# An attention and gated feed-forward layer on eight cores: the up-weight loads go from GpSimd's DMA queue to ScalarE's

## The chip, the cores and the metric

One Trainium2 chip, all eight cores. Each core takes one of the eight sequences (4096 tokens of 1024 features) through the whole layer by itself; the cores exchange nothing. The metric is the device time of the slowest core, in microseconds (us).

## The reference

```python
x = L0_attn_x                                  # (8, 4096, 1024), float32
xn = _layernorm(x, axis=-1)
s = attn(xn, Wq, bq, Wk, bk, Wv, bv, Wo, bo)   # 16 heads of 64, rotary q and k, causal softmax
# feed-forward, 3072 hidden; the weights are integers times 1/127
gate = einsum('bsd,hd->bsh', xn, w_gate / 127)
up   = einsum('bsd,hd->bsh', xn, w_up / 127)
h    = silu(gate) * up
g    = silu(einsum('bsh,dh->bsd', h, w_down / 127))
out  = x + s * g
```

## The kernel before

The kernel is written engine by engine: a small scheduler class (`Sched`) appends each instruction to its engine's list, with the semaphores that it waits for, and every DMA goes through one helper, so that all of them carry line 99 in the profile. An engine works through its list in the order written, and a DMA whose wait is not yet met holds up all that stands behind it in the list of the engine that issues it. SP, ACT and POOL issue DMAs. The helper's first argument names the issuing engine.

There are three parts.

1. Layer norm of x, 32 tiles of 128 tokens, transposed into `xnT`.
2. Attention for eight pairs of heads. In this part POOL also converts the integer feed-forward weights to bf16, in DRAM, into `wsc` (72 DMAs, 24 for each of gate, up and down).
3. The output projection, the feed-forward net and the final product, eight tiles of 512 tokens (`it`). This is the part that the change touches. Its SBUF tiles are carved out of `SCR` and `xnT`, and the profile calls them by these two names. In it the weights come from `wsc` by DMA, again for every token tile, each kind into a pair of slots:
   - gate weights of hidden chunk `hc` (256 KB, `wg_sl`), issued by ACT;
   - up weights (256 KB, `wu_sl`), issued by POOL;
   - the two halves of the down weights (128 KB each, `wdA_sl` and `wdB_sl`), issued by SP, which also loads x and stores the result.

Within one token tile the order is as follows.

- **Loop A**, 24 hidden chunks (lines 839 to 895). TensorE: 8 gate matmuls (L843), 8 up matmuls (L855), then the 4 first-half down matmuls of the chunk before (L824). ACT: SiLU of the gate (L865). DVE: product with up (L870). After them the slot just used is filled again, with chunk `hc + 2`: ACT issues the gate load once the gate matmuls of `hc` are done, and POOL the up load once its up matmuls are done. At chunk 12 two tiles of x are loaded for the next token tile (`emit_ln`, lines 757 to 788): SP issues the load, ACT normalizes (L767), TensorE transposes (L776), DVE copies (L784).
- Four SiLUs on ACT (L897) and four products on DVE (L903) empty the PSUM banks of the first half.
- **Loop B**, 24 chunks (lines 910 to 935): 4 second-half down matmuls each (L913), from `wdB_sl`, which SP fills two chunks ahead. At its chunks 0 and 1 `loadA` is called, which loads gate, up and first-half down weights of chunks 0 and 1 for the next token tile. Its last token tile has no such loads.
- Four SiLUs (L940) and products (L946), the output projection of the next token tile (L796, evicted by L804), transposes (L962), the sum with x (L970), the store, and two more tiles of layer norm.

Before the first token tile a fence is waited for, then the 2 MB of output-projection weights `wo_bf` are loaded by POOL (with a cast from float32), and `loadA(0)`, `loadA(1)`, `loadB(0)`, `loadB(1)` follow.

Each buffer has a record of who wrote and who read it last (`b_wu[sl].wr()` and the like); a load waits for these, and for the fence.

Of the kernel before, what the change touches and what calls it, by code (L numbers as in the profile page):

```python
# [119 lines left out]
def build_program(S):  # L120
# [23 lines left out]
    wsc = nc.dram_tensor("wsc", [3, NHC, 128, D], BF16, kind="Internal").ap()  # L144
# [3 lines left out]
    with stack:  # L148
# [48 lines left out]
        wu_sl = [SCR.ap()[:, 10240 + i * 1024:10240 + (i + 1) * 1024] for i in range(2)]  # L197
# [27 lines left out]
        wus_s = [sch.sem(f"wus{i}") for i in range(2)]  # L225
# [32 lines left out]
        b_wu = [B(), B()]  # L258
# [7 lines left out]
        DMA = sch.dma  # L266
# [26 lines left out]
        t = DMA("pool", wqs_s, wq_sl.rearrange("p (a c) -> p a c", a=NDC, c=128), rr(wq_l[0]))  # L293
        b_wq.setw(t)
        t = DMA("pool", wks_s, wk_sl.rearrange("p (a c) -> p a c", a=NDC, c=128), rr(wk_l[0]))
        b_wk.setw(t)
        wv4 = wv_sl.rearrange("p (a b c) -> p a b c", a=NDC, b=2, c=128)
        t = DMA("pool", wvs_s, wv4[:, :, 0, :], rr(wv_l[0]))
        b_wv.setw(t)
        t = DMA("pool", wvs_s, wv4[:, :, 1, :], rr(wv_l[1]))  # L300
# [6 lines left out]
        for rt in range(nRT):  # L307
            sl = rt % 3
# [8 lines left out]
                     after=b_xsl[sl].wr())  # L317
            b_xsl[sl].setw(xt)
            ts1 = E("dve", lambda v, s=sl, L=lnst_s: v.bn_stats(L[:, 0:6], xsl[s][:, 0:512]),
                    after=b_xsl[sl].rd(), signal=True)  # L320
            ts2 = E("dve", lambda v, s=sl, L=lnst_s: v.bn_stats(L[:, 6:12], xsl[s][:, 512:1024]),
                    after=b_xsl[sl].rd(), signal=True)
            agt = E("dve", lambda v, L=lnst_s, A=lnag_s: v.bn_aggr(A[:, :], L[:, :]),
                    after=(ts1, ts2) + b_lnag_s.wr(), signal=True)
# [3 lines left out]
                    after=(agt, cs_tok, eps_tok) + b_lnsq_s.wr(), signal=True)  # L328
# [3 lines left out]
                     after=(sqt,), signal=True)  # L332
# [4 lines left out]
                    after=(rct2,), signal=True)  # L337
# [5 lines left out]
                after=(stt,) + b_xsl[sl].rd() + b_xnb0[sl2].wr(), signal=True)  # L343
# [3 lines left out]
            for dc in range(NDC):  # L347
# [3 lines left out]
                    after=(cs_tok, xnbt) + (b_p0ps[sl2].wr() if dc == 0 else ()),  # L351
# [6 lines left out]
                after=(ptok,), signal=True)  # L358
# [317 lines left out]
        for g in range(NG):  # L676
# [15 lines left out]
            if g + 1 < NG:  # L692
# [5 lines left out]
                if g % 2 == 1:  # L698
                    tv = DMA("pool", wvs_s, wv4[:, :, 0, :], rr(wv_l[g + 1]),
                             after=b_wv.wr())  # L700
                    tv2 = DMA("pool", wvs_s, wv4[:, :, 1, :], rr(wv_l[g + 2]),
                              after=b_wv.wr())
# [11 lines left out]
        fence = sch.fence()  # L714
# [13 lines left out]
        def loadA(hc):  # L728
            sl = hc % 2
            t = DMA("act", wgs_s[sl], wg_sl[sl], wsc[0, hc], after=b_wg[sl].wr() + tuple(fence))  # L730
            b_wg[sl].setw(t)
            t = DMA("pool", wus_s[sl], wu_sl[sl], wsc[1, hc], after=b_wu[sl].wr() + tuple(fence))
            b_wu[sl].setw(t)
            t = DMA("sp", wdAs_s[sl], wdA_sl[sl], wsc[2, hc][:, 0:512],
                    after=b_wdA[sl].wr() + tuple(fence))
            b_wdA[sl].setw(t)

        def loadB(hc):
# [3 lines left out]
            b_wdB[sl].setw(t)  # L742

        loadA(0)
        loadA(1)
        loadB(0)
        loadB(1)
# [66 lines left out]
        for it in range(nIT):  # L814
# [6 lines left out]
            def emit_downA(job):  # L821
                hcj, slj, hpj = job
                for oc in range(4):
                    dt = E("pe", lambda te, h=hcj, o=oc, s=slj: te.matmul(  # L824
                        dn_ap[o][:, :], wdA_sl[s][:, o * 128:(o + 1) * 128],
                        hpr[:, h * 512:(h + 1) * 512],
                        start=(h == 0), stop=(h == NHC - 1), skip_group_check=True),
                        after=(hpj,) + b_wdA[slj].rd()
                        + (dn_b[oc].wr() if hcj == 0 else ()),
                        signal=(oc == 3))  # L830
                    if hcj == 0 and oc == 3:
                        for o2 in range(4):
                            dn_b[o2].setw(dt)
                    elif hcj == NHC - 1 and oc == 3:
                        for o2 in range(4):
                            dn_b[o2].addw(dt)
                    b_wdA[slj].addr(dt)

            for hc in range(NHC):
                sl = hc % 2  # L840
                gt = None
                for dc in range(NDC):
                    gt = E("pe", lambda te, d=dc, s=sl, x_=xnt_c: te.matmul(  # L843
                        gateb[:, :], wg_sl[s][:, d * 128:(d + 1) * 128],
                        x_[:, d * 512:(d + 1) * 512],
                        start=(d == 0), stop=(d == NDC - 1), skip_group_check=True),
                        after=b_wg[sl].rd() + b_xntc.rd()
                        + (b_S6[0].wr() if dc == 0 else ()),
                        signal=(dc == NDC - 1))
                b_S6[0].setw(gt)  # L850
                b_wg[sl].addr(gt)
                b_xntc.addr(gt)
                ut = None
                for dc in range(NDC):
                    ut = E("pe", lambda te, d=dc, s=sl, x_=xnt_c: te.matmul(  # L855
                        upb[:, :], wu_sl[s][:, d * 128:(d + 1) * 128],
                        x_[:, d * 512:(d + 1) * 512],
                        start=(d == 0), stop=(d == NDC - 1), skip_group_check=True),
                        after=b_wu[sl].rd() + b_xntc.rd()
                        + (b_S6[1].wr() if dc == 0 else ()),  # L860
                        signal=(dc == NDC - 1))
                b_S6[1].setw(ut)
                b_wu[sl].addr(ut)
                b_xntc.addr(ut)
                sg = E("act", lambda sc: sc.activation(  # L865
                    sgb[:, :], gateb[:, :], AF.Silu, scale=1.0 / 127.0),
                    after=(gt,) + b_sgb.wr(), signal=True)
                b_S6[0].addr(sg)
                b_sgb.setw(sg)
                hp = E("dve", lambda v, h=hc: v.tensor_mul(  # L870
                    hpr[:, h * 512:(h + 1) * 512], sgb[:, :], upb[:, :]),
                    after=(sg, ut) + b_hpr.wr(), signal=True)
                b_S6[1].addr(hp)
                b_sgb.addr(hp)
                b_hpr.addw(hp)
                if dn_pend is not None:
                    emit_downA(dn_pend)
                    nhc = dn_pend[0] + 2
                    if nhc < NHC:
                        slw = nhc % 2  # L880
                        t = DMA("sp", wdAs_s[slw], wdA_sl[slw], wsc[2, nhc][:, 0:512],
                                after=b_wdA[slw].wr() + tuple(fence))
                        b_wdA[slw].setw(t)
                dn_pend = (hc, sl, hp)
                if hc + 2 < NHC:
                    slw = (hc + 2) % 2
                    t = DMA("act", wgs_s[slw], wg_sl[slw], wsc[0, hc + 2],
                            after=b_wg[slw].wr() + tuple(fence))
                    b_wg[slw].setw(t)
                    t = DMA("pool", wus_s[slw], wu_sl[slw], wsc[1, hc + 2],  # L890
                            after=b_wu[slw].wr() + tuple(fence))
                    b_wu[slw].setw(t)
                if hc == 12 and it + 1 < nIT:
                    emit_ln(it + 1, rps=(0, 1))
            emit_downA(dn_pend)
            for oc in range(4):
# [3 lines left out]
                    after=dn_b[oc].rd() + b_gbf.wr(), signal=True)  # L900
# [5 lines left out]
                    after=(g2,) + b_st.rd() + b_prod.wr(), signal=True)  # L906
# [3 lines left out]
            for hc in range(NHC):  # L910
                sl = hc % 2
                for oc in range(4):
# [4 lines left out]
                        after=b_hpr.rd() + b_wdB[sl].rd()  # L917
# [20 lines left out]
            for oc in range(4):  # L938
# [4 lines left out]
                    after=dn_b[oc].rd() + b_gbf.wr(), signal=True)  # L943
# [5 lines left out]
                    after=(g2,) + b_st.rd() + b_prod.wr(), signal=True)  # L949
# [5 lines left out]
            for rp in range(4):  # L955
# [5 lines left out]
                for oc in range(NDC):  # L961
# [4 lines left out]
                        after=b_prod.rd() + (bb.wr() if oc == 0 else ()),  # L966
# [5 lines left out]
                    after=(tt,) + b_xp6[slot].rd() + b_xp6[slot].wr(), signal=True)  # L972
# [102 lines left out]
```

How the kernel before makes its waits and increments, by code:

```python
            def body(engine, ops=ops):  # L109
                for fn, waits, incs in ops:
                    for sem, val in waits:
                        engine.wait_ge(sem, val)
                    ins = fn(engine)
                    for sem, n in incs:
                        ins.then_inc(sem, n)
```

## Time and profile before

| | us |
|---|---|
| median of the 2 timed runs | 4350.02 (4340.29 and 4359.75) |
| profiled execution, its own time | 4203.06 |
| its span, slowest core (core 0) | 4201.5 |
| spans of the other seven cores | 4164.7 to 4188.5 |
| mean granted TensorE clock of core 0 | 0.864 |

The profiled execution was 3.4% shorter than the median of the timed runs. All rows of the trace belong to the profiled one; its time is its span and 1.56 us around it. A row of the timeline reads: start, duration, engine, line, operation, tiles, count, and in brackets how long the engine had been idle and what it waited for. ACTq and SPq are DMA issues on those engines; on POOL they stand under POOL itself.

### The profile page before, as it was taken

Reading aid. Unit: us, or ns where it says so; the run is one execution under the profiler, and the core shown is the slowest. Engines: PE = TensorE matmul, PEld = TensorE weight load, DVE = VectorE, ACT = ScalarE, POOL = GpSimd, SP = SyncE. Lnnn points to the kernel's source line nnn. Section 1 sums busy time; section 2 is a strip of 40 time slices with the busy share of each in tenths; the row PEclk is TensorE's granted clock in tenths of the full one; section 3 lists DMA queues with packets and bytes.
Section 4 is the critical chain, followed back from the end, with each engine's and each line's share of the span. In section 5 each row is a group of like instructions: output and inputs, shape, how many; then the busy total and the mean of one; then the engine's idle time right before and its main releaser. Section 6 shows DMA issues by size and latency. Waiting matters only on the chain.

```text
span 4201.5 us, 38240 instructions; the slowest of 8 cores (4164.7 to 4201.5 us)
## 1 busy us (share of the span) xinstructions
PE 2800.9 (67%) x12576; PEld 1132.2 (27%) x12800; DVE 770.2 (18%) x1600; ACT 1495.6 (36%) x1475; POOL 186.1 (4%) x309
## 2 busy tenths in 40 slices
PE   1176656676656776556766664778786968787787
PEld 1132211231211231111412211333242424333332
DVE  3331131121221211210210310111111111111111
ACT  2226626546446356256266265211111111111111
POOL 0000010000000000000000000000000101000000
PEclk9997967988868878878978787899998989999999
DMA  4230040030030210300400002434342424343443
GB/s 116 76 48 0 2 51 1 13 36 0 15 38 1 33 15 1 43 10 0 60 12 1 20 0 41 105 100 136 100 144 95 144 94 135 108 128 109 122 123 103
DMA packets 208942, 250.07 MB, mean 60 GB/s; under 512 B 101584, under 2 KB 150736, under 8 KB 208112
## 3 DMA queue, kind: packets, MB, share of 16 engines
q0 software_dynamic: 99696, 79.79, 11.5%
q1 hardware_dynamic: 81408, 117.49, 8.9%
q10 hardware_dynamic: 27648, 50.34, 4.2%
q8 instruction: 109, 1.79, 0.2%
q14 instruction: 81, 0.66, 0.1%
HBM read 241.25 MB, written 35.65 MB: 66 GB/s over the span
## 4 chain that ended last, share of the span: by engine, by line
PE 45%; ACT 25%; DMA 11%; DVE 8%; issue 8%; SPq 3%; ACTq 0%; DVEq 0%; POOL 0%; POOLq 0%
ACT SCR L584 12%; PE S L564 9%; PE S L843 8%; ACT SCR L598 8%; PE S L855 8%; DMA SCR<-wsc 5%; DMA SCR<-SCR 3%; PE C L639 3%; PE C L440 3%; PE S L824 3%; SPq L99 2%; PE S L796 2%; PE S L913 2%; DMA SCR<-x 1%; ACT rct L486 1%
## 5 line engine op out<-in xcount | busy, mean ns | idle before, releaser
L564 PE MATMUL S<-SCR 64*128 64x512 bf16 (+3 forms) x2304 | 448.1, 438 | 601.5 <-ACT SCR L584 266.4
L584 ACT ACTIVATE SCR<-S 128x3072 bf16<-128x3072 f32 x224 | 611.7, 2731 | 308.5 <-PE S L564 308.5
L639 PE MATMUL C<-SCR 128*128 128x512 bf16 (+3 forms) x2208 | 614.4, 416 | 129.0 <-DVE ctxT L502 61.6
L598 ACT ACTIVATE SCR<-S 128x1536 bf16<-128x1536 f32 (+3 forms) x320 | 381.4, 1195 | 452.3 <-PE S L564 442.4
L843 PE MATMUL S<-xnT,SCR 128*128 128x512 bf16 x1510 | 380.4, 395 | 4.2 <-issue 1.5
L564 PEld LDWEIGHTS S<-SCR 64*128 64x128 bf16 x2304 | 130.0, 102 | 913.6 <-issue 876.9
L865 ACT ACTIVATE xnT<-S 128x512 bf16<-128x512 f32 x192 | 114.6, 597 | 731.3 <-PE S L843 718.0
L392 PE MATMUL S<-xnT,SCR 128*128 128x512 bf16 x1007 | 280.2, 440 | 130.7 <-DVE SCR L400 127.9
L855 PE MATMUL S<-xnT,SCR 128*128 128x512 bf16 x1496 | 363.0, 383 | 2.1
L639 PEld LDWEIGHTS C<-SCR 128*128 128x128 bf16 x2304 | 207.6, 106 | 516.7 <-issue 400.8
L613 DVE TENSOR_TENSOR SCR<-SCR,tri_s 128x128 bf16<-128x128 bf16 x512 | 81.0, 220 | 1215.6 <-ACT SCR L598 1215.3
L913 PE MATMUL S<-xnT,SCR 128*128 128x512 bf16 x560 | 171.3, 411 | 142.1 <-DMA SCR<-wsc 118.9
L870 DVE TENSOR_TENSOR xnT<-xnT,S 128x512 bf16<-128x512 bf16 x192 | 132.1, 688 | 698.3 <-PE S L855 692.5
L843 PEld LDWEIGHTS S<-xnT,SCR 128*128 128x128 bf16 x1536 | 155.3, 102 | 192.5 <-issue 24.9
L855 PEld LDWEIGHTS S<-xnT,SCR 128*128 128x128 bf16 x1536 | 152.0, 99 | 187.6 <-issue 11.5
L392 PEld LDWEIGHTS S<-xnT,SCR 128*128 128x128 bf16 x1024 | 109.6, 110 | 298.6 <-issue 221.2
L99 POOL DMA_DIRECT2D SCR<-wsc x192 | 103.5, 539 | 1420.1 <-PE S L855 1353.0
L796 PE MATMUL S<-ctxT,SCR 128*128 128x512 bf16 x497 | 122.4, 404 | 51.1 <-DMA SCR<-wo_l 30.8
L824 PE MATMUL S<-xnT,SCR 128*128 128x512 bf16 x562 | 152.6, 379 | 2.4 <-DVE xnT L870 1.8
L348 PE MATMUL S<-id_s,ctxT 128*128 128x128 bf16 x256 | 32.4, 307 | 178.5 <-ACT ctxT L340 178.5
L502 DVE TENSOR_TENSOR ctxT<-ceb,C 64x512 bf16<-64x512 bf16 x128 | 87.0, 680 | 309.8 <-PE C L496 299.0
L457 ACT ACTIVATE SCR<-C 128x128 bf16<-128x128 f32 x128 | 35.9, 281 | 297.3 <-PE C L446 297.3
(78 smaller groups left out, 1758.0 us busy)
## 6 DMA issues: line engine op xcount, KB each, us to landing
SCR<-wsc ACTq DMA_DIRECT2D x192, 256.0 KB, 2.7
SCR<-wsc SPq DMA_DIRECT2D x384, 128.0 KB, 2.8
SCR<-wsc POOLq DMA_DIRECT2D x192, 256.0 KB, 3.2
ctxT<-x SPq DMA_DIRECT2D x32, 512.0 KB, 3.6
SCR<-SCR SPq DMA_DIRECT2D x256, 64.0 KB, 2.0
SCR<-x SPq DMA_DIRECT2D x32, 512.0 KB, 4.2
out<-SCR SPq DMA_DIRECT2D x32, 512.0 KB, 2.8
wsc<-wg_l POOLq DMA_DIRECT2D x24, 256.0 KB, 14.1
```

The source lines that it names most:

```text
L99: return self.emit(eng, lambda e, o=out, i=in_: e.dma_start(out=o, in_=i), after=after, signal=sem, inc=16)
L392: mmt = E("pe", lambda te, i=it, d=dc, r=reg, w=w_ap: te.matmul(r[:, :], w[:, d * 128:(d + 1) * 128], xnT.ap()[:, d * S + i * 512: d * S + ...
L564: S_=Sreg, i_=it, kl=klo: te.matmul(S_[0:128, o:o + w_], Kg[kl:kl + 64, j * 128:(j + 1) * 128], Qg[kl:kl + 64, i_ * 512 + r_: i_ * 512 + r ...
L584: etok = E("act", lambda sc, P_=Pb: sc.activation(P_[:, 0:3072], S6.ap()[:, 0:3072], AF.Exp, scale=0.125), after=(specs[0][9], specs[1][9] ...
L598: etok = E("act", lambda sc, w_=wexp, h_=h2, P_=Pb: sc.activation(P_[:, h_ * 1536: h_ * 1536 + w_], S6.ap()[:, h_ * 1536: h_ * 1536 + w_], ...
L639: sp=(is_diag and kk == len(grp) - 1): te.matmul(C_.ap()[0:128, r_:r_ + w_], Vt[:, j * 130 + v_: j * 130 + v_ + 128], P_[:, h_ * 1536 + o: ...
L796: mt = E("pe", lambda te, o=oc, d=dc, r=reg, i=it: te.matmul(r[:, :], wo_bf[:, o * 1024 + d * 128: o * 1024 + (d + 1) * 128], ctxT.ap()[:, ...
L824: dt = E("pe", lambda te, h=hcj, o=oc, s=slj: te.matmul(dn_ap[o][:, :], wdA_sl[s][:, o * 128:(o + 1) * 128], hpr[:, h * 512:(h + 1) * 512] ...
L843: gt = E("pe", lambda te, d=dc, s=sl, x_=xnt_c: te.matmul(gateb[:, :], wg_sl[s][:, d * 128:(d + 1) * 128], x_[:, d * 512:(d + 1) * 512], s ...
L855: ut = E("pe", lambda te, d=dc, s=sl, x_=xnt_c: te.matmul(upb[:, :], wu_sl[s][:, d * 128:(d + 1) * 128], x_[:, d * 512:(d + 1) * 512], sta ...
L870: hp = E("dve", lambda v, h=hc: v.tensor_mul(hpr[:, h * 512:(h + 1) * 512], sgb[:, :], upb[:, :]), after=(sg, ut) + b_hpr.wr(), signal=True)
L913: dt = E("pe", lambda te, h=hc, o=oc, s=sl: te.matmul(dn_ap[o][:, :], wdB_sl[s][:, o * 128:(o + 1) * 128], hpr[:, h * 512:(h + 1) * 512], ...
```

## The change

Two DMAs name ACT in place of POOL: the up-weight load in `loadA`, and the one in loop A for chunk `hc + 2`. Slots, semaphores, sizes and waits stay as they were.

```diff
@@ loadA(hc)
             t = DMA("act", wgs_s[sl], wg_sl[sl], wsc[0, hc], after=b_wg[sl].wr() + tuple(fence))
             b_wg[sl].setw(t)
-            t = DMA("pool", wus_s[sl], wu_sl[sl], wsc[1, hc], after=b_wu[sl].wr() + tuple(fence))
+            t = DMA("act", wus_s[sl], wu_sl[sl], wsc[1, hc], after=b_wu[sl].wr() + tuple(fence))
             b_wu[sl].setw(t)
@@ loop A
                     b_wg[slw].setw(t)
-                    t = DMA("pool", wus_s[slw], wu_sl[slw], wsc[1, hc + 2],
+                    t = DMA("act", wus_s[slw], wu_sl[slw], wsc[1, hc + 2],
                             after=b_wu[slw].wr() + tuple(fence))
```

On POOL, the end of the program before: the loads of the last attention pair's weights, the last conversions, the projection weights and all the up loads.

```order
L99 DMA SCR<-wq_l 128x8x128
L99 DMA SCR<-wk_l 128x8x128
L99 DMA wsc<-wd_l 16x8192 x18
L99 DMA SCR<-wo_l 128x64x128
L99 DMA SCR<-wsc 128x1024 x192
L1009 UNCONDITIONAL_BRANCH
```

And now:

```order
L99 DMA SCR<-wq_l 128x8x128
L99 DMA SCR<-wk_l 128x8x128
L99 DMA wsc<-wd_l 16x8192 x18
L99 DMA SCR<-wo_l 128x64x128
L1009 UNCONDITIONAL_BRANCH
```

The 192 up loads have gone from POOL, and nothing else; POOL has no work after `wo_l`.

On ACT, from the end of attention to the first chunk of loop A, before (`SCR<-wsc 128x1024` are gate loads):

```order
L486 ACTIVATE rct<-C 1x512
L490 ACTIVATE rct<-rct 1x512
L99 DMA SCR<-wsc 128x1024 x2
L804 ACTIVATE xnT<-S,bos 128x512 x8
L767 ACTIVATE xnT<-SCR,lnbi,lnsc 128x1024 x4
L865 ACTIVATE xnT<-S 128x512
L99 DMA SCR<-wsc 128x1024
```

And now, where `SCR<-wsc 128x1024` are gate and up loads by turns:

```order
L486 ACTIVATE rct<-C 1x512
L490 ACTIVATE rct<-rct 1x512
L99 DMA SCR<-wsc 128x1024 x4
L804 ACTIVATE xnT<-S,bos 128x512 x8
L767 ACTIVATE xnT<-SCR,lnbi,lnsc 128x1024 x4
L865 ACTIVATE xnT<-S 128x512
L99 DMA SCR<-wsc 128x1024 x2
```

The up loads of chunks 0 and 1 stood behind `wo_l` on POOL; they now stand on ACT, which has no `wo_l` ahead of them. In each chunk of loop A one load behind the SiLU has become two.

On ACT, the end of loop A, loop B and what follows, before:

```order
L865 ACTIVATE xnT<-S 128x512
L99 DMA SCR<-wsc 128x1024
L865 ACTIVATE xnT<-S 128x512 x2
L897 ACTIVATE xnT<-S 128x512 x3
L897 ACTIVATE xnT<-C 128x512
L99 DMA SCR<-wsc 128x1024 x2
L940 ACTIVATE xnT<-S 128x512 x3
L940 ACTIVATE xnT<-C 128x512
```

And now:

```order
L865 ACTIVATE xnT<-S 128x512
L99 DMA SCR<-wsc 128x1024 x2
L865 ACTIVATE xnT<-S 128x512 x2
L897 ACTIVATE xnT<-S 128x512 x3
L897 ACTIVATE xnT<-C 128x512
L99 DMA SCR<-wsc 128x1024 x4
L940 ACTIVATE xnT<-S 128x512 x3
L940 ACTIVATE xnT<-C 128x512
```

The up loads of the next token tile's chunks 0 and 1 stood on POOL directly behind the last up load of loop A; they now stand behind the four L897, with the gate loads.

## Rows read from the trace of the kernel before

**Rows 1.** The page's head.

```profile
span 4201.5 us, 38240 instructions; the slowest of 8 cores (4164.7 to 4201.5 us)
```

**Rows 2.** The page's chain that ended last.

```profile
PE 45%; ACT 25%; DMA 11%; DVE 8%; issue 8%; SPq 3%; ACTq 0%; DVEq 0%; POOL 0%; POOLq 0%
ACT SCR L584 12%; PE S L564 9%; PE S L843 8%; ACT SCR L598 8%; PE S L855 8%; DMA SCR<-wsc 5%; DMA SCR<-SCR 3%; PE C L639 3%; PE C L440 3%; PE S L824 3%; SPq L99 2%; PE S L796 2%; PE S L913 2%; DMA SCR<-x 1%; ACT rct L486 1%
```

**Rows 3.** Busy time by stretch: inside one loop A, then one loop B.

```profile
core 0: us, PE busy (x) PEld busy (x) DVE busy (x) ACT busy (x) POOL busy (x), PEclk, DMA share, GB/s
3060.00:3170.00 110.00, 100.10 (x459) 45.84 (x467) 17.22 (x25) 15.75 (x25) 12.40 (x23) 0.95 0.49 140
3175.00:3215.50 40.50, 25.66 (x90) 8.12 (x93) 0.42 (x1) 0.07 (x1) 0.00 (x0) 0.88 0.30 91
```

**Rows 4.** The page's groups: busy, mean ns | idle before, releaser.

```profile
L855 PE MATMUL S<-xnT,SCR 128*128 128x512 bf16 x1496 | 363.0, 383 | 2.1
...
L913 PE MATMUL S<-xnT,SCR 128*128 128x512 bf16 x560 | 171.3, 411 | 142.1 <-DMA SCR<-wsc 118.9
```

**Rows 5.** Line 99's issues: ns min/median/max, first and last start.

```profile
L99 ACTq DMA_DIRECT2D SCR<-wsc x192: 325/326/741, 2603.7 to 4128.3; - x192
L99 POOL DMA_DIRECT2D SCR<-wsc x192: 537/539/566, 2607.2 to 4130.3; - x192
```

**Rows 6.** The page's DMA issues: KB each, median us from issue to landing.

```profile
SCR<-wsc ACTq DMA_DIRECT2D x192, 256.0 KB, 2.7
...
SCR<-wsc POOLq DMA_DIRECT2D x192, 256.0 KB, 3.2
```

**Rows 7.** Timeline, one chunk of loop A.

```profile
2673.99 0.60 ACT L865 ACTIVATE xnT<-S 128x512 bf16<-128x512 f32 x1 [3.72 <-PE S L843]
2674.06 0.33 ACTq L99 DMA_DIRECT2D SCR<-wsc  x1
...
2676.05 0.54 POOL L99 DMA_DIRECT2D SCR<-wsc  x1 [3.78 <-PE S L855]
2676.21 1.89 PE L843 MATMUL S<-xnT,SCR 128*128 128x512 bf16 x8
...
2678.31 0.60 ACT L865 ACTIVATE xnT<-S 128x512 bf16<-128x512 f32 x1 [3.72 <-PE S L843]
```

**Rows 8.** Around the start of loop B in five token tiles; DMA rate, 3175 to 3216.

```profile
2788.71 1.44 PE L913 MATMUL S<-xnT,SCR 128*128 128x512 bf16 x3 [1.62 <-DMA SCR<-wsc]
3168.98 0.54 POOL L99 DMA_DIRECT2D SCR<-wsc  x1 [3.78 <-PE S L855]
3174.55 0.81 ACTq L99 DMA_DIRECT2D SCR<-wsc  x2
3179.00 1.44 PE L913 MATMUL S<-xnT,SCR 128*128 128x512 bf16 x3 [1.50 <-DMA SCR<-wsc]
3769.14 1.44 PE L913 MATMUL S<-xnT,SCR 128*128 128x512 bf16 x3 [2.69 <-DMA SCR<-wsc]
3966.06 1.44 PE L913 MATMUL S<-xnT,SCR 128*128 128x512 bf16 x3 [1.39 <-DMA SCR<-wsc]
4148.21 1.44 PE L913 MATMUL S<-xnT,SCR 128*128 128x512 bf16 x3 [0.73 <-DMA SCR<-wsc]
GB/s 52 370 182 227 188 5 39 89 120 8 81 95 80 26 113 117 0 128 128 0 121 134 1 72 132 52 0 136 120 0 125 130 1 89 141 26 16 134 106 0
```

**Rows 9.** The load of the projection weights; the last row is core 3's wait.

```profile
2604.45 2.80 POOL L99 DMA_DIRECT2D SCR<-wo_l  x1 [531.69 <-DVE ctxT L502]
2633.62 16.25 PE L796 MATMUL S<-ctxT,SCR 128*128 128x512 bf16 x63 [30.83 <-DMA SCR<-wo_l]
  DMA SCR<-wo_l: 23.4, 1
```

**Rows 10.** Timeline at chunk 12 of loop A.

```profile
3109.08 0.54 POOL L99 DMA_DIRECT2D SCR<-wsc  x1 [3.78 <-DMA SCR<-wsc]
3110.21 0.81 SPq L99 DMA_DIRECT2D SCR<-x  x2
3115.61 1.24 ACT L767 ACTIVATE xnT<-SCR,lnbi,lnsc 128x1024 bf16<-128x1024 f32 x1 [7.99 <-DMA SCR<-x]
```

## Prediction

> **What bounds the kernel now.** I read the page's head first: a span of 4201.5 us on the slowest core, the other seven within 1% of it [rows 1]. Then the chain that ended last: TensorE holds 45%, ACT 25%, DMA 11%, and POOL and its queue 0% [rows 2]. Two of its entries lie in the part that changes and could be touched: the waits for transfers out of `wsc` (5%) and those for x (1%). The ACT entries (L584, L598) belong to attention, which issues the same instructions as before.
>
> Next the stretches. In 110 us of loop A TensorE is busy for 100.1, its granted clock is 0.95, and the DMA engines are busy half the time (0.49). In a loop B of 40.5 us it is busy for only 25.7 [rows 3]. The groups say what each stretch waits for: the up matmuls L855 were idle for 2.1 us before all 1496 of them, the loop B matmuls L913 for 142.1 us, of which 118.9 us waited for DMA [rows 4]. So the up loads, which the change moves, are never waited for where they are used; the transfers that TensorE does wait for are the second-half down weights of loop B. The question is where the up loads go, and whom they meet there.
>
> **Part 1: the issue itself, 192 times.** An issue takes 326 ns on ACT and 539 ns on POOL [rows 5]. ACT gets 192 x 0.326 = 62.6 us of extra queue time. It is hidden. One chunk of loop A lasts 4.32 us (from one SiLU at 2673.99 to the next at 2678.31), of which ACT uses 0.60 for the SiLU and 0.33 for the gate load, and sits idle for 3.72 between the SiLUs, the issue falling into that gap [rows 7]. If that cover were gone the cost would be the whole 62.6 us (1.5%). POOL saves 192 x 0.539 us, which nobody waited for: 0.
>
> **Part 2: the wait that ACT now makes.** The up load waits for the up matmuls of the same chunk. Behind it on ACT stands the next chunk's SiLU, which waits for the next chunk's gate matmuls, and these stand behind those up matmuls on TensorE. ACT would wait until about 2676.0, issue until 2676.4, and the SiLU is due at 2678.31: 1.9 us to spare [rows 7]. At chunk 12 the normalization of x stands behind it: the up load can be issued at about 3109.1, and the normalization starts at 3115.61, when x has landed [rows 10]. Cost 0 in both places.
>
> **Part 3: does an up load land in time?** It is issued at 2676.05; the up matmuls that use it begin two chunks after those that freed the slot. The next chunk's gate starts at 2676.21, its up matmuls after 8 matmuls at about 2678.0, and the chunk that needs the load 4.32 us later, at 2682.3: 6.2 us to land [rows 7]. A 256 KB load landed in 2.7 us from ACT and in 3.2 us from POOL [rows 6]. Nothing is late, nothing is gained. Were both loads of a chunk to land one behind the other, that would be 5.4 us, still in time.
>
> **Part 4: the two up loads for the next token tile.** Here the move matters. On POOL they had nothing ahead of them, so they went out as soon as the slots were free, at the end of loop A; the later of the two at 3168.98. ACT can issue them only behind its four L897, at 3174.55 and after, with the two gate loads [rows 8]. That is the beginning of loop B, where TensorE soon needs the second-half down weights of chunk 2, issued by SP when chunk 0 is done. The trace holds a comparison. Seven loops B have the two gate loads at their start, the eighth has none. The seven first waits for DMA run from 1.62 us in the first token tile to 1.39 us in the seventh, with 1.50 and a longest of 2.69 between them; their mean is 1.74. In the eighth it is 0.73 [rows 8]. Two 256 KB loads thus cost about 1.0 us of waiting. Two more should cost as much again: 7 x 1.0 = +7 us. The bounds: nothing, if the loads are through before the down weights are asked for; and the pure transfer, 512 KB at the highest rate seen there, 370 GB/s [rows 8], is 1.4 us, so 10 us for seven. Twice the steepest reading (2.69 - 0.73 = 2.0 per token tile) would be 7 x 2.0 = 14 us, and I take that as the upper end. A late chunk 2 moves all that follows, since each later load is issued when an earlier chunk is done, so the delay is not won back. The value that I take is +7, since it is measured on the same loads at the same place.
>
> A second effect there is that a longer gap could change TensorE's clock. Directly after the four L897 three matmuls take 1.44 us in the row at 3179.00, at the lower of the two levels, and the mean over this loop B is 0.88 [rows 3, 8]. The slow stretch exists already with and without the gate loads (the row at 4148.21 has it too), so I add nothing, and let up to 1 us a token tile stand in the range.
>
> **Part 5: the start of this part of the kernel.** TensorE stands still for 30.83 us until the projection weights have landed; on core 3 the same wait is 23.4 us [rows 9]. The up loads of chunks 0 and 1 stood behind this load on POOL. Now they go out ahead of it on ACT and share the DMA engines with it: 512 KB at 370 GB/s is +1.4 us. Below, 0, if the weights' many small packets leave room; above, the spread between the cores, 7.4 us. I take +1.4.
>
> **Part 6: chunk 12.** The x load is issued at 3110.21 and lands 5.4 us later, while TensorE and ACT wait [rows 10]. An up load runs beside it in both kernels. Issued from ACT it starts at most half a microsecond sooner and landed 0.5 us faster (2.7 against 3.2) [rows 6], so x could land up to 0.5 us earlier, 7 x 0.5 = -3.5 us; if instead the up load's 256 KB now take more of the engines' turns, x is late by 0.7 us, +5 us. I take 0.
>
> The Trainium skill says something that bears on parts 3 and 6: the page DMA: Bandwidth & Descriptors, section Latency and other measured facts, gives about 0.6 us to the first byte of a DMA issued by ACT or SP and about 1 us for one issued by GpSimd. The 0.5 us between the two landings in this trace agrees. By that rule alone the sum would be an estimated 7 x 0.4 = 3 us lower, if x gained all of it.
>
> **The sum.** +7 + 1.4 = +8.4 us on the profiled execution's own time of 4203.06, or 0.2%. A measurement of this kernel can tell about 2% from no change, so this is no change. The two timed runs were 4340.29 and 4359.75, 3.4% above the profiled one, at the same work; the trace does not show why. The forecast is for the timed median: 4350.02 + 8.4, about 4358 us.
>
> **The rivals.**
>
> *A. No cost at all, or a small gain.* The wait at the head of loop B grows by nothing, since the gate loads and up loads are through in time, and x lands earlier: between -3.5 and +1.4 us, 4347 to 4351. For it: ACT issues all four by about 3176.2, while the down weights are asked for at about 3175.9 and the rate there is far below its peak soon after [rows 8]. Against it: two loads alone already cost 1.0 us.
>
> The Trainium skill has a rule for a gain: the page SBUF — State Buffer, section Who interferes with whom, says that DVE operations in some of its fast modes keep GpSimd from writing its DMA descriptors, and advises to issue from ACT or SP. Here the POOL issues take 537 to 566 ns, all 192 of them, so no such blocking shows [rows 5], and the up loads are not waited for anyway. By this rule the sum would stay as it is.
>
> *B. Slower: the shared ACT queue makes loads late in loop A.* Gate load and up load of a chunk now follow each other in one queue, beside SP's. The place is the up matmuls of each chunk from 2 on, 22 in a token tile, 176 in all. It decides from a landing of over 6.2 us (part 3). With 0.5 us of lateness each, TensorE would lose 88 us, 2.1%: 4438. In its favour is only that half of the DMA time is taken in loop A [rows 3]; against it is that this load stays the same, that landings are half of what is allowed, and that L855 has waited for 2.1 us in all.
>
> *C. ACT as the bound.* If the 1.9 us to spare of part 2 went, each extra issue would delay a SiLU, 62.6 us: 4413. Against it: 3.72 us of idle time in 4.32 [rows 7].
>
> *D. Faster by over 2%.* That would need 84 us. All waits for `wsc` before L913 together are 118.9 us [rows 4], and the up loads take no part in them in loop B beyond its start. Nothing in the rows gives it.
>
> **How the numbers follow.** The forecast, a small loss of 2 to 20 us: 0.62. A: 0.28. B: 0.04. C: 0.02. D: 0.02. The remaining 0.02 is that the program loses by something that I don't see. C stays within 2%. Of each of the first two cases I leave a little for runs that differ by more than the change does (they differ by 3.4% already between timed and profiled). That gives faster 0.04, same 0.90, slower 0.06. The mechanism alone would allow a range from 4345 to 4380. The level adds more than that: if the time after is taken at the level of the profiled execution, it is 4203 + 8 = 4211, with A's gain 4200. I cannot exclude it, so the range goes from 4200 to 4390.
>
> **What would show each step right or wrong.** Part 1 and 2: 384 issues out of `wsc` on ACT at about 326 ns, none on POOL; the gap ahead of L865 still ended by the gate matmuls, the chunk still 4.32 us. Part 3: idle time before L843 and L855 still a few us in all. Part 4: the first DMA wait of loop B at about 2.7 us in seven token tiles and 0.7 in the eighth, and L913's DMA wait up from 118.9 to about 126 us. Part 5: the wait for `wo_l` up by 1 to 2 us. Part 6: the wait of L767 for x the same within 5 us. I am wrong if L913's wait stays where it is (A), if L855 has waits for DMA (B), or if anything in attention differs.

## The result and the profile after

| | before | after |
|---|---|---|
| median of all runs, us | 4207.28 (21 runs, 4190.77 to 4414.48) | 4213.39 (22 runs, 4204.54 to 4370.81) |
| profiled execution, its own time | 4203.06 | 4210.64 |
| its span, slowest core | 4201.5 (core 0) | 4209.1 (core 6) |

Ratio after to before 1.0023, 95% interval 1.0013 to 1.0032: slower by 0.23%, 9.7 us on 4207.28. That is no change by the 2% that one measurement can tell, but clear of noise with this many runs. In some executions of either kernel the cores of one die run at a lower granted clock and take up to 5% longer, and by their times both runs of before that the forecast was built on (4340.29 and 4359.75) were of that kind; the ratio leaves such runs out.

The page after has the same span to 0.2%, and the up loads have moved from POOL to ACT:

```profile
span 4209.1 us, 38226 instructions; the slowest of 8 cores (4183.5 to 4209.1 us)
PE 2799.8 (67%) x12576; PEld 1131.5 (27%) x12800; DVE 769.8 (18%) x1600; ACT 1495.7 (36%) x1475; POOL 82.3 (2%) x117
...
L855 PE MATMUL S<-xnT,SCR 128*128 128x512 bf16 x1496 | 361.0, 381 | 2.1
...
L913 PE MATMUL S<-xnT,SCR 128*128 128x512 bf16 x560 | 170.2, 409 | 149.6 <-DMA SCR<-wsc 126.7
...
SCR<-wsc ACTq DMA_DIRECT2D x384, 256.0 KB, 2.7
```

The reader sees first what did not change. The up matmuls L855 waited for 2.1 us in all, as before [rows 4], so the moved loads still arrive in time. L913, the matmuls of loop B, now wait for DMA for 126.7 us where it was 118.9 [rows 4]. Over the eight cores of each profile that sum went from 114.3 to 118.9 (mean 116.9) up to 121.1 to 132.0 (mean 127.9): +11.0 us a core.

The timeline says where. Below stand one chunk of loop A, then the start of loop B in the first token tile, and the first wait for a down load in the last token tile, all on core 6 of after:

```profile
2673.37 0.60 ACT L865 ACTIVATE xnT<-S 128x512 bf16<-128x512 f32 x1 [3.72 <-DMA SCR<-wsc]
2673.44 1.86 ACTq L99 DMA_DIRECT2D SCR<-wsc  x2
...
2677.68 0.60 ACT L865 ACTIVATE xnT<-S 128x512 bf16<-128x512 f32 x1 [3.72 <-DMA SCR<-wsc]
...
2784.19 1.78 ACTq L99 DMA_DIRECT2D SCR<-wsc  x4
...
2790.31 1.44 PE L913 MATMUL S<-xnT,SCR 128*128 128x512 bf16 x3 [3.26 <-DMA SCR<-wsc]
...
4156.42 1.44 PE L913 MATMUL S<-xnT,SCR 128*128 128x512 bf16 x3 [0.96 <-DMA SCR<-wsc]
```

A chunk of loop A lasts 4.31 us, against 4.32 [rows 7], and ACT sits idle for the same 3.72 us ahead of each SiLU. At the head of loop B four loads go out in a row, and the first wait for a down load is 3.26 us where it was 1.62 [rows 8]. In the eighth loop B, which has no loads for a next token tile, it is 0.96. Read over all cores (54 first waits found in the profile of after, 53 of before, in the seven token tiles that have such loads), the mean went from 1.69 to 3.12 us: 7 x 1.43 = 10.0 us, which is nearly the whole of the 11.0. In the eighth tile it was 0.67 in both. The down load itself shows it too: the first one that SP issues in loop B, whose landing ends this wait, lands on average 3.18 us after its issue in before and 4.62 in after, and 2.1 in the eighth tile of both. Behind that wait the loops differ by only 0.3 us each, so the delay is not won back and hardly grows.

A caution for reading: the releaser named for the gap ahead of L865 turned from the gate matmuls into DMA (553.0 us of such waits in after's groups). It is the same 3.72 us gap, ended at the same moment.

### The profile page after: what moved, and what is told of

Same layout as the page of the kernel before. It is cut to its first block, busy times and chain, and to the rows that moved or that the text cites. A ratio compares the mean times of both kernels' runs of the same rounds, so it can differ in the third digit from the quotient of the medians.

```text
span 4209.1 us, 38226 instructions; the slowest of 8 cores (4183.5 to 4209.1 us)
## 1 busy us (share of the span) xinstructions
PE 2799.8 (67%) x12576; PEld 1131.5 (27%) x12800; DVE 769.8 (18%) x1600; ACT 1495.7 (36%) x1475; POOL 82.3 (2%) x117
## 4 chain that ended last, share of the span: by engine, by line
PE 45%; ACT 25%; DMA 11%; issue 8%; DVE 8%; SPq 3%; ACTq 0%; DVEq 0%; POOL 0%; POOLq 0%
ACT SCR L584 12%; PE S L564 9%; PE S L843 8%; ACT SCR L598 8%; PE S L855 8%; DMA SCR<-wsc 5%; DMA SCR<-SCR 3%; PE C L639 3%; PE C L440 3%; PE S L824 3%; SPq L99 2%; PE S L796 2%; PE S L913 2%; DMA SCR<-x 2%; PE S L392 1%
## 5 line engine op out<-in xcount | busy, mean ns | idle before, releaser
L865 ACT ACTIVATE xnT<-S 128x512 bf16<-128x512 f32 x192 | 114.7, 597 | 727.1 <-DMA SCR<-wsc 553.0
L855 PE MATMUL S<-xnT,SCR 128*128 128x512 bf16 x1496 | 361.0, 381 | 2.1
L913 PE MATMUL S<-xnT,SCR 128*128 128x512 bf16 x560 | 170.2, 409 | 149.6 <-DMA SCR<-wsc 126.7
L855 PEld LDWEIGHTS S<-xnT,SCR 128*128 128x128 bf16 x1536 | 151.3, 99 | 185.5 <-issue 7.6
L940 ACT ACTIVATE xnT<-S 128x512 bf16<-128x512 f32 x24 | 14.3, 597 | 348.8 <-PE C L913 337.8
```

Of the source, the lines that this page charges most:

```text
L855: ut = E("pe", lambda te, d=dc, s=sl, x_=xnt_c: te.matmul(upb[:, :], wu_sl[s][:, d * 128:(d + 1) * 128], x_[:, d * 512:(d + 1) * 512], sta ...
L913: dt = E("pe", lambda te, h=hc, o=oc, s=sl: te.matmul(dn_ap[o][:, :], wdB_sl[s][:, o * 128:(o + 1) * 128], hpr[:, h * 512:(h + 1) * 512], ...
```

## The experiments

Theory 1 is that the cost sits at the head of loop B, where the number of 256 KB loads ahead of the second-half down loads went from two to four. Theory 2 is that it comes from gate and up loads sharing a queue all through loop A, which would show where x is waited for. The table gathers eight of the ten runs; the other two, e9 and e10, repeat e7 and e4 for a closer time and stand further below. "L913" and "x" are the mean over eight cores of what L913 waited for transfers from `wsc` and L767 for x. "Loops B" is the sum of the eight stretches from the first L897 to the first L940, the mean of eight cores. "First wait" is the mean of those of the first seven token tiles. "Core mean" is the mean of all cores' spans over the runs that the ratio uses, less the same for before on the same chip, with its standard error.

| kernel | loads at the head | L913, us | first wait, us | loops B, us | x, us | ratio to before (95%) | core mean, us |
|---|---|---|---|---|---|---|---|
| before | 2 gate | 116.9 | 1.69 | 364.6 | 103.7 | | |
| after | 2 gate, 2 up | 127.9 | 3.12 | 376.7 | 107.8 | 1.0023 (1.0013 to 1.0032) | |
| e8, after again | 2 gate, 2 up | 125.5 | 2.98 | 375.2 | 107.6 | 1.0037 (1.0021 to 1.0053) | +16.0 ± 2.3 |
| e1, loop A part | 2 gate | 117.1 | 1.61 | 363.7 | 106.1 | 1.0006 (0.9978 to 1.0033) | +1.5 ± 2.3 |
| e2, head part | 2 gate, 2 up | 126.6 | 3.12 | 376.3 | 102.8 | 1.0003 (0.9966 to 1.0041) | +6.5 ± 2.1 |
| e3, swapped | 2 up | 117.5 | 1.69 | 364.5 | 107.3 | 1.0001 (0.9977 to 1.0025) | +1.7 ± 2.4 |
| e5, ups early | 2 gate | 116.1 | 1.72 | 364.6 | 106.6 | 1.0008 (0.9967 to 1.0049) | +2.3 ± 3.0 |
| e4, all early | none | 110.9 | 0.66 | 354.6 | 106.8 | 0.9969 (0.9940 to 0.9999) | -10.8 ± 1.8 |
| e7, gates early | none | 109.1 | 0.63 | 353.7 | 104.0 | 0.9983 (0.9946 to 1.0020) | -10.0 ± 2.2 |
| e6, spread | none; 4 later in loop B | 114.2 | 0.72 | 364.1 | 105.3 | 0.9988 (0.9974 to 1.0002) | -1.1 ± 1.7 |

**The two halves of the change, each alone.** e1 moves only the loads inside loop A. (Since one semaphore serves one kind of issuer here, the up loads of `loadA` got a pair of their own, `hd_s`.)

```diff
+        hd_s = [sch.sem(f"hd{i}") for i in range(2)]
@@ loadA: stays on POOL
-            t = DMA("pool", wus_s[sl], wu_sl[sl], wsc[1, hc], after=...)
+            t = DMA("pool", hd_s[sl], wu_sl[sl], wsc[1, hc], after=...)
@@ loop A
-                    t = DMA("pool", wus_s[slw], wu_sl[slw], wsc[1, hc + 2],
+                    t = DMA("act", wus_s[slw], wu_sl[slw], wsc[1, hc + 2],
```

> Only the 176 up loads inside loop A are issued by ACT; the two up loads for the next token tile stay on POOL, at the end of loop A. Theory 1 (the cost sits at the head of loop B, where four 256 KB loads instead of two are ahead of the second-half down weights): ratio to before 1.000, within 0.9990 to 1.0010; first DMA wait of loop B 1.6 to 1.7 us as before (3.1 with the change), the sum of L913's waits for DMA 117 us a core as before (128 with the change). Theory 2 (gate and up loads in one queue disturb loop A, seen in the later landing of x at chunk 12, 104 to 108 us of waiting): ratio 1.002, first wait of loop B unchanged, L767's wait for x 108 us.

e2 moves only the ones in `loadA`:

```diff
+        hd_s = [sch.sem(f"hd{i}") for i in range(2)]
@@ loadA
-            t = DMA("pool", wus_s[sl], wu_sl[sl], wsc[1, hc], after=...)
+            t = DMA("act", hd_s[sl], wu_sl[sl], wsc[1, hc], after=...)
```

> Only the up loads for the next token tile (and those of chunks 0 and 1 at the start) are issued by ACT, behind the four L897; inside loop A they stay on POOL. Theory 1: the whole cost of the change, ratio 1.002 to 1.003; first DMA wait of loop B 3.1 us in seven token tiles and 0.65 in the eighth, L913's waits 128 us. Theory 2: ratio 1.000 and L767's wait for x 104 us.

The start of the first loop B on the slowest core of e1:

```profile
2771.43 0.81 ACTq L99 DMA_DIRECT2D SCR<-wsc  x2
...
2775.90 1.44 PE L914 MATMUL S<-xnT,SCR 128*128 128x512 bf16 x3 [1.54 <-DMA SCR<-wsc]
```

The same place in e2:

```profile
2778.43 1.77 ACTq L99 DMA_DIRECT2D SCR<-wsc  x4
...
2783.46 1.44 PE L914 MATMUL S<-xnT,SCR 128*128 128x512 bf16 x3 [2.20 <-DMA SCR<-wsc]
```

Two issues and 1.54 us against four issues and 2.20. (2.20 is among the shortest first waits of e2, which go down to 2.16; their mean is 3.12, as with the whole change.) e1, with 176 of the change's 192 loads, leaves loops B as they were; e2, with the other 16, of which 14 sit at a head, has the whole of their lengthening. The ratios cannot tell the two kernels apart, since their intervals reach 0.3 to 0.4% to either side; the core means, +1.5 and +6.5 us, go the way of theory 1 but are only some two errors apart. They add up to 8 us, with an error of about 4, where the whole change had +16.0 ± 2.3 on another chip (e8). The verdict rests on the waits. Theory 2 keeps one thing: x is waited for 106.1 us in e1 and 102.8 in e2, so what makes x later is the part in loop A. The seven waits at chunk 12 alone, where the up loads run beside x, come to 47.1 us a core in before, 47.4 in e2 and 50.9 in e1, so this part costs 4 us of waiting.

**Which loads, or how many?** e3 is the change with the gate loads of `loadA` on POOL, which issues them at the end of loop A, so that the two loads at the head are the up loads.

```diff
+        hd_s = [sch.sem(f"hd{i}") for i in range(2)]
@@ loadA of the changed kernel
-            t = DMA("act", wgs_s[sl], wg_sl[sl], wsc[0, hc], after=...)
+            t = DMA("pool", hd_s[sl], wg_sl[sl], wsc[0, hc], after=...)
```

> The change, but the two gate loads for the next token tile are issued by POOL, which has nothing ahead of them, so they go out at the end of loop A; the two up loads stay on ACT behind the four L897. Two loads are at the head of loop B, as before, but of the other kind. Theory 1 (the number of loads there counts, not their kind or the mix of queues): ratio 1.000, first DMA wait 1.6 to 1.7 us, L913's waits 117 us. Theory 2: ratio 1.002, as with the change.

The second loop B of its slowest core, with the two gate loads on POOL ahead of it and the two up loads on ACT at its head:

```profile
2964.12 0.54 POOL L99 DMA_DIRECT2D SCR<-wsc  x1 [193.85 <-PE S L844]
...
2968.43 0.54 POOL L99 DMA_DIRECT2D SCR<-wsc  x1 [3.78 <-PE S L844]
...
2975.73 0.81 ACTq L99 DMA_DIRECT2D SCR<-wsc  x2
...
2980.64 1.44 PE L914 MATMUL S<-xnT,SCR 128*128 128x512 bf16 x3 [1.95 <-DMA SCR<-wsc]
```

Loops B 364.5 us, first wait 1.69 on average: as before. The number counts, not the kind.

**Queue or moment?** e5 keeps the up loads on ACT and only writes them ahead of the four L897.

```diff
@@ between loop A and the four L897 of the changed kernel
             emit_downA(dn_pend)
+            if it + 1 < nIT:
+                loadU(0)
+                loadU(1)
@@ loop B; loadA without its up load, which is now loadU
                 if hc == 0 and it + 1 < nIT:
-                    loadA(0)
+                    loadA(0, False)
                 if hc == 1 and it + 1 < nIT:
-                    loadA(1)
+                    loadA(1, False)
```

> The change, but the two up loads for the next token tile are written ahead of the four L897, still on ACT; gate and first-half down loads stay at the head of loop B. It has the change's queue with the place in time of before. Theory 1 (the number of loads at the head of loop B): first DMA wait 1.6 to 1.7 us in seven token tiles, L913's waits 117 us a core, loops B 364 us in all, ratio to before 1.000 to 1.001. Rival (the up loads on ACT's queue cost wherever they are issued): L913's waits 127 us, ratio 1.002.

The start of the first loop B on its slowest core, with the four SiLUs at L905 here:

```profile
2762.08 1.86 ACTq L99 DMA_DIRECT2D SCR<-wsc  x2
...
2765.76 0.60 ACT L905 ACTIVATE xnT<-S 128x512 bf16<-128x512 f32 x1 [3.16 <-PE C L829]
...
2769.63 0.81 ACTq L99 DMA_DIRECT2D SCR<-wsc  x2
...
2774.29 1.44 PE L921 MATMUL S<-xnT,SCR 128*128 128x512 bf16 x3 [1.70 <-DMA SCR<-wsc]
```

L913's waits 116.1 us, loops B 364.6. With the same queue and the old moment the whole cost in loop B is gone, so it was the moment. The rival had 127.

**Nothing at the head.** e4 writes all of `loadA` ahead of the L897. With the four gate and up loads this also moves the two 128 KB first-half down loads, which SP issues.

```diff
@@ of the changed kernel
             emit_downA(dn_pend)
+            if it + 1 < nIT:
+                loadA(0)
+                loadA(1)
@@ loop B
-                if hc == 0 and it + 1 < nIT:
-                    loadA(0)
-                if hc == 1 and it + 1 < nIT:
-                    loadA(1)
```

> The change, but gate, up and first-half down loads for the next token tile are written ahead of the four L897, so ACT and SP issue them at the end of loop A. No load is left at the head of loop B. Theory 1: the first DMA wait of all eight loops B falls to 0.65 us, 7 x (3.1 - 0.65) = 17 us less than with the change and 7 us less than before: ratio to before 0.998; L913's waits about 110 us. A rival (the order on ACT matters: the wait for the last up matmuls now stands ahead of L897 and delays it): loop B starts later by what ACT waits, ratio 1.000 or above, and the gap ahead of L897 grows from 3.16 us. Theory 2: ratio 1.002 at least.

The first loop B of its slowest core:

```profile
2774.26 1.86 ACTq L99 DMA_DIRECT2D SCR<-wsc  x4
...
2777.95 0.60 ACT L900 ACTIVATE xnT<-S 128x512 bf16<-128x512 f32 x1 [3.16 <-PE C L824]
...
2785.13 1.25 PE L916 MATMUL S<-xnT,SCR 128*128 128x512 bf16 x3 [0.50 <-DMA SCR<-wsc]
```

The issues stand ahead of the first of the four SiLUs (L900 here, L897 in the listing), whose gap is 3.16 us as in after, so the rival of a delayed SiLU is out. The first wait falls to 0.66 us on average, against 3.12 with four loads at the head and 1.69 with two, and loops B fall by 22.1 us against after. e7 is the same edit made to the kernel before, with the up loads on POOL throughout.

> The kernel before (up loads on POOL), with gate and first-half down loads for the next token tile written ahead of the four L897. Nothing is left at the head of loop B, and loop A has its up loads on POOL. Theory 1: first wait 0.65 us, L913's waits 111 us, ratio 0.997. With it, if the up loads on ACT are what makes x late at chunk 12 (103 us of waiting in both kernels with POOL there, 106 to 108 in four with ACT), L767's wait for x is 103 us, and this kernel is the fastest of all, some 3 us below the one with all loads early on ACT.

It did what theory 1 says: 109.1 us, 353.7 us, and x at 104.0 us. That it would be some 3 us faster than e4 was not shown; the two core means, -10.0 and -10.8, are equal within their errors. Both were run again for a closer time.

> The same kernel as e7_gates_early, for a closer time. Theory 1: ratio to before 0.997 to 0.998 (7 us less waiting in L913, loops B 11 us shorter). Rival: the shorter loop B is given back elsewhere and the ratio is 1.000.

> The same kernel as e4_all_early (up loads on ACT throughout, none at the head of loop B). Theory 1: ratio 0.997 to 0.998. If the later x at chunk 12 counts (107 against 104 us of waiting), it is some 0.0007 above e9_gates_early_again, which the rounds would hardly tell.

Measured: e9 0.9987 (0.9962 to 1.0012), core mean -8.7 ± 2.2 us; e10 0.9995 (0.9969 to 1.0021), core mean -5.6 ± 2.3 us. Neither of these two ratios is clear of 1, nor is that of e7, and that of e4 (0.9940 to 0.9999) only just, so the slowest core's time does not show a gain with any certainty. The four core means (-10.8, -10.0, -8.7, -5.6) agree in sign, each more than two errors from zero. Writing the loads early beats the kernel before by 0.1 to 0.3% on the mean of the cores, as far as these runs tell, which is far below the 2% that one measurement can tell.

**Bunched or spread?** e6 has SP issue the four gate and up loads at chunks 4, 8, 12 and 16 of loop B.

```diff
@@ loop B of the changed kernel; loadWdA is the down part of loadA
-                if hc == 0 and it + 1 < nIT:
-                    loadA(0)
-                if hc == 1 and it + 1 < nIT:
-                    loadA(1)
+                if it + 1 < nIT and hc in (0, 1):
+                    loadWdA(hc)
+                if it + 1 < nIT and hc in (4, 8, 12, 16):
+                    loadGU((hc // 4 - 1) % 2, (hc // 4 - 1) // 2)
```

> The change, but the four gate and up loads for the next token tile are issued by SP, one each behind the second-half down load of chunks 4, 8, 12 and 16 of loop B. The head of loop B is free of them, but all four still run inside it. If only the bunch at the head costs: first wait 0.65 us, L913's waits 111 us as with all loads early, ratio 0.997. If each 256 KB load costs TensorE about its own transfer time (0.7 us) wherever it meets loop B's chain of down loads: first wait 0.65 us, but L913's waits 111 + 7 x 4 x 0.6 = 128 us, ratio 1.002, as with the change.

Neither extreme held. The head was free (0.72 us), but loops B took 364.1 us, 9.5 to 10.4 more than with all loads early: 28 loads at 0.34 us each, against 22.1 / 28 = 0.79 us each when four stand bunched. Bunched, a 256 KB load costs loop B twice as much as alone. The two costs are not of one kind. Of the 22.1 us, 17.0 are L913's waits for DMA; of the 9.5 us only 3.3 are, and in the rest TensorE is busy longer with the same matmuls (L913 busy for 220.3 us a core in e6, 213.9 in e4; granted clock over the loops B 0.914 and 0.926). The 128 KB first-half down loads, which e6 leaves at the head and e4 moves, hardly matter: the first wait is 0.72 us with them there and 0.66 without. e6 also changes the issuing engine to SP, and no run separates that from the spreading.

**The change once more**, next to these:

> The changed kernel as it is, on the same chip as the others, as their yardstick: ratio 1.002 to 1.003, first wait 3.1 us, L913's waits 128 us.

1.0037 (1.0021 to 1.0053), L913 125.5 us, first wait 2.98: the first measurement repeats, at the upper side. Its core mean, +16.0 ± 2.3 us, is also above the 9.7 us of the first.

## Why the prediction was right or wrong

**The level: wrong.** The step that failed is the last of the sum, "The forecast is for the timed median: 4350.02 + 8.4, about 4358 us". The median of before over 21 runs is 4207.28, within 0.1% of the profiled execution, and that of after is 4213.39. The text had seen the 3.4% between two timed runs and the profiled one, and that the trace does not explain them; it then took the two for the kernel's time, though every term of the sum came from the trace of the profiled one. Built on the profiled time, as its own sum was, the forecast is 4211.5. The range, widened to 4200 for just this doubt, held the time. And a forecast of 4358 said of a kernel that runs in 4207 would mean 3.6% slower, which nothing in the working supports.

**The difference: right in sign and size.** Forecast +8.4 us (0.2%), measured +0.23% (0.13 to 0.32), 9.7 us. That the two are so close is partly luck: the head of loop B cost more than its term, x cost what had been put at 0, the projection weights cost nothing, and a gain that the sum did not have made up for part of it. By its terms:

- *Part 1, ACT's extra issues at no cost: held.* 384 issues on ACT, the gap ahead of the SiLU still 3.72 us, the chunk 4.31 us.
- *Part 2, the wait for the up matmuls delays nothing on ACT: held*, also in e4, where the wait stands ahead of the four SiLUs of the first half and their gap stays 3.16 us.
- *Part 3, up loads in time: held.* L855 waited for 2.1 us in all.
- *Part 4, the head of loop B: the mechanism is shown* by e1, e2, e3, e4 and e5. The term was too small. It took the second pair of loads to cost what the first did, 1.0 us a token tile. The first pair costs 1.69 - 0.66 = 1.0, the second 3.12 - 1.69 = 1.43, or 10 us in all instead of 7. The down load that ends the wait lands after 2.15 us with no load at the head (e4), 3.18 with two (before) and 4.62 with four (after). The first pair is issued by 3175.4 in before, half a microsecond ahead of the down load that TensorE will wait for; the second goes out beside it and after it. The stated upper bound of a pure transfer at 370 GB/s (1.4 us) was the better guess. What the text calls twice the steepest reading, 2.69 - 0.73 = 2.0 us, is that reading once; it bounded the range only.
- *Part 4's clock term, nothing: too simple, and the effect lay elsewhere.* In the loops B, L913's waits rose by 11.0 us and the loops by 12.1, so about 1 us is left for a slower clock. But the seven stretches between loops B (L940 of a token tile to L897 of the next) took 1038.4 us in after against 1040.9, although x was waited for 4 us longer in them. The granted clock over these stretches was 0.925 in after and 0.921 in before (mean of eight cores, errors 0.001). Over the kernels the length follows it: 1036.0 us at 0.925 in e2, 1037 at 0.924 in e6, 1039.6 at 0.922 in e7, but 1043 to 1045 us at 0.919 to 0.920 in e1, e3 and e5. So a little more clock goes with what came back. Why it was granted stays open: after and e2, whose loops B are the longest, have it, but so has e4 (0.924), whose loops B are short.
- *Part 5, projection weights +1.4 us: wrong, it was 0.* The wait over eight cores was 26.1 us before and 26.2 after, with a spread of 7 us in before alone. The two up loads ahead of `wo_l` did not push it back by a measurable amount.
- *Part 6, x at chunk 12 at 0: wrong, +4 us of waiting.* The wait for x rose from 103.7 to 107.8 us a core, near the +5 end that the text gave. The whole rise is at chunk 12, where seven waits went from 47.1 to 51.4 us; the other waits for x are 56.6 and 56.4. It is 102.8 in e2 and 104.0 in e7, which have POOL issue the up loads in loop A, and 105.3 to 107.6 in e1, e3 to e6 and e8, which have ACT issue them.

At chunk 12 in after:

```profile
3109.90 1.86 ACTq L99 DMA_DIRECT2D SCR<-wsc  x2
...
3113.02 0.84 SPq L99 DMA_DIRECT2D SCR<-x  x2
...
3118.72 1.24 ACT L767 ACTIVATE xnT<-SCR,lnbi,lnsc 128x1024 bf16<-128x1024 f32 x1 [8.29 <-DMA SCR<-x]
```

Here ACT's normalization starts 5.7 us after the issue of x; in before it was 5.4 [rows 10]. Over all cores a load of x at chunk 12 lands 4.84 us after its issue in before and 5.33 in after, and the wait for it goes from 6.7 to 7.3 us: 7 x 0.6 = 4.3 us. The idea that a faster up load clears the way for x was the wrong way round: through ACT it lands sooner (2.7 against 3.2 us [rows 6]) and x later. Why was not tried.

Of the rivals, A (no cost, the loads are through in time) fell with the first wait of 3.12 us; B (late up loads) and C (ACT as the bound) had nothing in the trace for them and did not come, nor did D (a gain of 2%). The Trainium skill, page DMA: Bandwidth & Descriptors, section Latency and other measured facts, would have had the sum an estimated 3 us lower by its earlier first byte; the landings agree with it (2.7 us from ACT, 3.2 from POOL), but x, which was to gain by it, was waited for 4.1 us longer. The Trainium skill's page SBUF — State Buffer, section Who interferes with whom, has a rule for a gain from leaving GpSimd; no run here shows one.

## What to carry to other kernels

When a DMA moves to another engine's queue, ask first what stands ahead of it there: two of the loads of each token tile went out 7 to 10 us later than before and so met a loop that waits for one small load after another, which cost 10 us; the other 22 cost 4 us of waiting for x. A transfer that nobody waits for can still be the one that makes another late; look for a stretch of the same loop without it in the trace (here the last token tile) and read the price off. And before a forecast is put on a level, ask why the timed runs and the profiled one differ: two runs that lie 3.4% above the trace are no level for a change of 0.2%.

## What the runs showed of the hardware

A 256 KB load beside a chain of 128 KB loads, each waited for, lengthened the chain's loop by 0.34 us when it came alone (e6 against e4) and by 0.79 us when four were bunched at its head (after against e4). At that head the first wait grew by 1.0 us with the first two loads and by 1.43 us with the next two, and the 128 KB load waited for took 2.15, 3.18 and 4.62 us to land with none, two and four of them. What the bunched loads fetch made no difference (e3); whether the engine that issues the bunch matters was not tried. The up loads landed half a microsecond sooner from ACT than from POOL (2.7 against 3.2 us), and a 512 KB load of SP issued behind them took half a microsecond more to land (5.33 against 4.84 us).
